# Softmax shifts of the second attention per half batch: maxima three head groups ahead, split on GpSimd

## What is computed

```python
q = x @ w_q + b_q                  # x: 16 batches, 256 queries, 128 channels
k = context @ w_k + b_k            # context: 1601 keys of 96 channels
v = context @ w_v + b_v
scores = einsum('bqhd,bkhd->bhqk', q, k) * 8 ** -0.5     # 16 heads of 8 channels
weights = softmax(scores, axis=-1)
out = einsum('bhqk,bkhd->bqhd', weights, v).reshape(16, 256, 128)
return out @ w_o + b_o
```

## Time and profile before

| | us |
|---|---|
| median of 3 runs | 2914.64 |
| lowest and highest run | 2913.44, 2914.93 |
| the profiled execution | 2913.21 |
| its span, first to last instruction | 2911.2 |
| VectorE busy | 2192.4 (75%) |
| TensorE busy | 2405.5 (83%) |
| ScalarE busy | 2106.3 (72%) |
| GpSimd busy | 1248.6 (43%) |

### The profile page before, as it was taken

One profiled execution on the slowest core, in us unless ns is written; L12 is line 12 of the kernel. 1 busy time (PEld: TensorE's weight loads), 2 busy tenths in 40 slices (PEclk: granted clock), 3 DMA queues, 4 the chain that ended last, 5 costly groups with the idle time before them and its releaser, 6 DMA issues. The chain is left out here.

```text
span 2911.2 us, 60895 instructions
## 1 busy us (share of the span) xinstructions
PE 2405.5 (83%) x19797; PEld 1252.2 (43%) x19797; DVE 2192.4 (75%) x8041; ACT 2106.3 (72%) x3547; POOL 1248.6 (43%) x1593
## 2 busy tenths in 40 slices
PE   7958888888888888667788479999999999999638
PEld 5735555555555555534522123333333333333337
DVE  8739878888888878636645799999999999993313
ACT  5749889898988888714412058888999888889325
POOL 1428777777777777713200412222322222200154
PEclk9979889988998899788888579999999999999669
DMA  8820000000000000081341113344443433330222
GB/s 245 266 79 12 13 14 15 14 13 14 13 18 19 14 15 14 5 290 55 51 117 35 68 49 104 89 98 108 106 104 95 105 89 97 95 68 2 59 93 68
DMA packets 163460, 205.76 MB, mean 71 GB/s; under 512 B 78588, under 2 KB 131106, under 8 KB 163126
## 3 DMA queue, kind: packets, MB, share of 16 engines
q1 hardware_dynamic: 152774, 161.80, 21.6%
q0 software_dynamic: 10352, 39.92, 4.0%
HBM read 135.19 MB, written 66.60 MB: 69 GB/s over the span
## 5 line engine op out<-in xcount | busy, mean ns | idle before, releaser
L2148 ACT ACTIVATE pb<-sps 128x512 f32<-128x512 f32 (+1 forms) x1664 | 896.1, 597 | 187.9 <-PE sps L2090 174.0
L2173 DVE TENSOR_REDUCE mx<-wps 128x2 f32<-128x1024 f32 x768 | 885.4, 1217 | 41.3 <-PE wps L2063 32.3
L1076 DVE MAX8 cand<-sc 128x8 f32<-128x46 f32 (+1 forms) x4480 | 602.7, 199 | 136.8 <-issue 77.9
L2105 PE MATMUL ops<-pb,va 128*9 128x256 f32 x6656 | 515.5, 382 | 8.2 <-issue 2.8
L852 PE MATMUL scores<-ctxT,qT 97*128 97x512 f32 (+1 forms) x1024 | 437.2, 576 | 80.5 <-ACT sc L964 69.5
L852 PEld LDWEIGHTS scores<-ctxT,qT 97*128 97x128 f32 x1024 | 206.6, 212 | 318.4 <-issue 218.6
L1943 POOL COPY va<-XX 128x128 f32<-128x128 f32 (+1 forms) x208 | 49.9, 292 | 626.0 <-PE ops L2105 618.4
L735 POOL TENSOR_TENSOR prf<-sc,prf 128x1601 f32<-128x1601 f32 x64 | 229.7, 3589 | 127.0 <-ACT prf L971 127.0
L827 PE MATMUL misc<-diag,prs 128*128 128x128 f32 (+1 forms) x1664 | 237.9, 300 | 7.0 <-issue 5.9
L735 POOL TENSOR_TENSOR prs<-sc,prs 128x1601 f32<-128x1601 f32 x64 | 230.6, 3604 | 16.8 <-ACT prs L971 13.8
L827 PEld LDWEIGHTS misc<-diag,prs 128*128 128x128 f32 (+1 forms) x1664 | 217.1, 207 | 17.3 <-issue 13.9
(11 more groups left out here) (407 smaller groups left out, 3953.5 us busy)
## 6 DMA issues: line engine op xcount, KB each, us to landing
FO<-keys SPq DMA_DIRECT2D x392, 50.0 KB
XX<-keys SPq DMA_DIRECT2D x392, 50.0 KB
ctxn<-in_ctx_dram SPq DMA_DIRECT2D x32, 576.0 KB
keys<-kpb POOLq DMA_DIRECT2D x42, 400.2 KB, 3.8
toep<-kernpad SPq DMA_DIRECT2D x8, 2048.0 KB, 14.9
values<-s_vs SPq DMA_DIRECT2D x16, 832.0 KB, 5.9
XX<-values SPq DMA_DIRECT2D x16, 832.0 KB, 4.8
keysf<-s_kf SPq DMA_DIRECT2D x16, 800.5 KB, 3.7
```

The source lines that it names most:

```text
L1076: st.add(v.max(cand[s % 2][:, 8 + n:8 + n + 7 * NP + 1:NP], sc[s % 4][:, c:c + w]))
L2105: ins = t.matmul(ops[VW * i:VW * i + DH1 + 1, 0:S], va[par][0:kn(kt), kt, 4 * g + i, :], pb[(UNITS * g + 2 * kt + i % 2) % 8][0:kn(kt), i ...
L2148: nc.scalar.activation(pb[(UNITS * g + u) % 8][0:rows_, :, :], sps[(UNITS * g + u) % SB][0:rows_, :, :], ACT.Exp).then_inc(p_ready, 1)
L2173: v.tensor_reduce(mx4[:, m // 2, :, 2 * g + m % 2, c], both, AX.X, ALU.max).then_inc(work_read, 1)
```

## The change

The maxima run three head groups ahead of the scores. In a batch's first group these are the last group of the same batch, in its other groups the first three of the next one; three groups of maxima run ahead of batch 0 and the last three groups of batch 15 have none beside them. The shifts are put in per half batch (two head groups): a half's split starts at the beginning of a batch's second group (for its own second half) and of its fourth group (for the next batch's first half), and one guard job stands at key tile 5 of each. VectorE only reduces `mx4` to `mneg` (half as many elements); the three casts and two subtractions are GpSimd's. TensorE turns both 128-query halves in one job, VectorE copies them to `mT` in one instruction of 256 columns on 24 partitions, and SyncE writes and reads back half the rows, twice per batch. In GpSimd's queue the split of a batch's second half stands between the spreading of the values and the splitting of the keys, the next one behind the splitting of the keys. In SyncE's queue the guard of the second half stands ahead of a batch's first loads. The scores wait for guard rows at the first and at the third group of a batch. Ahead of the loop, the split stands at the start of the third group and its guard job behind the fifth of that group's 13 jobs.

```diff
-                    mg = (g + 1) % HG
-                    ahead = 1 if g < HG - 1 else 2
-                    beside = follow >= ahead
-                    if g == HG - 1 and follow >= 1:
-                        do.split_maxima(b + 1)
+                    mg = (g + 3) % HG
+                    ahead = 0 if g == 0 else 1
+                    beside = ahead == 0 or follow
+                    half = 2 * b + (g + 1) // 2
+                    guarded = g == 1 or (g == 3 and follow)
+                    if guarded:
+                        do.split_maxima(half)
...
-                        if g == HG - 1 and follow >= 1 and kt in (5, 6):
-                            job(do.guard, b, par, b + 1, kt - 5)
+                        if guarded and kt == 5:
+                            job(do.guard, b, par, half)
...
-            for g in range(HG + 1):
+            for g in range(3):
                 for n in range(MJ):
-                    if g == HG and n == MJ // 2:
+                    if g == 2 and n == 0:
                         do.split_maxima(0)
-                    num = g * MJ + n
-                    do.maxima(g // HG, g // HG, 1, *job_args(g % HG, n), n == 0, num, wps[num % 2])
-            for q in range(2):
-                num = (HG + 1) * MJ + q
-                do.guard(0, q, num, wps[num % 2])
+                    num = g * MJ + n + (1 if g == 2 and n >= 5 else 0)
+                    do.maxima(0, 0, 1, *job_args(g, n), n == 0, num, wps[num % 2])
+                    if g == 2 and n == 4:
+                        do.guard(0, num + 1, wps[(num + 1) % 2])
...
+            def split_maxima(half):
+
+                pool.wait_ge(mneg_ready, half + 1)
+                pool.sem_inc(pool_passed, 1)
+                rest = mneg[:, :, :, :]
+                for n in range(3):
+                    st.link(g_.tensor_copy(mparts[:, :, n, :, :], rest))
+                    if n < 2:
+                        st.link(g_.tensor_tensor(rest, rest, mparts[:, :, n, :, :], ALU.subtract))
+                st.restart()
+                pool.sem_inc(mparts_ready, 1)
...
+            split_maxima(0)
+            split_keys(2)
+            split_maxima(1)
+            split_keys(3)
+            split_maxima(2)
+            for b in range(1, B - 1):
+                spread_values(b + 1, (b + 1) % 2)
+                split_maxima(2 * b + 1)
+                if b + 3 < B:
+                    split_keys(b + 3)
+                split_maxima(2 * b + 2)
+            split_maxima(2 * B - 1)
...
             def batch(b, par):
 
+                guard(2 * b + 1)
                 for g in range(HG - 2):
                     load(b + 2, par, g)
                 load_values(b + 2, True)
-                guard(b + 1, 1 - par, not (isinstance(b, int) and b == 0))
+                guard(2 * b + 2)
                 for g in range(HG - 2, HG):
                     load(b + 2, par, g)
...
-                if g == 0 and kt == 0:
-                    pe.wait_ge(guard_in, 32 * (b + 1))
+                if g % 2 == 0 and kt == 0:
+                    pe.wait_ge(guard_in, 32 * (2 * b + g // 2 + 1))
...
-            def split_maxima(b):
+            def split_maxima(half):
 
                 dve.wait_ge(work_read, maxima.last + 1)
-                rest = mneg[:, :, :, :]
-                st.link(v.tensor_reduce(rest.rearrange("p q o h -> p (q o h)"),
-                                        mx4[:, :, :, :, :].rearrange("p q o h c -> p (q o h) c"), AX.X, ALU.max, negate=True))
-                for n in range(3):
-                    st.link(v.tensor_copy(mparts[:, :, n, :, :], rest))
-                    if n < 2:
-                        st.link(v.tensor_tensor(rest, rest, mparts[:, :, n, :, :], ALU.subtract))
-                dve.sem_inc(mparts_ready, 1)
+                pairs = mx4[:, :, :, HP * (half % 2):HP * (half % 2) + HP, :]
+                v.tensor_reduce(mneg[:, :, :, :].rearrange("p q o h -> p (q o) h"),
+                                pairs.rearrange("p q o h c -> p (q o) h c"), AX.X, ALU.max, negate=True
+                                ).then_inc(mneg_ready, 1)
```

More of the change, by code:

```diff
@@ L1842, in base @@
                 return START
-            return START + PER * b - 3 - (MJ if isinstance(b, int) and b == B - 1 else 0)
+            return START + PER * b - 3
         def job_slot(b, par, n):
@@ L1893, in batch @@
                                 job(do.output, b, par, b - 1)
-                        if g == HG - 1 and follow >= 1 and kt in (5, 6):
-                            job(do.guard, b, par, b + 1, kt - 5)
+                        if guarded and kt == 5:
+                            job(do.guard, b, par, half)
                 do.batch_end()
-            for g in range(HG + 1):
+            for g in range(3):
                 for n in range(MJ):
-                    if g == HG and n == MJ // 2:
+                    if g == 2 and n == 0:
                         do.split_maxima(0)
-                    num = g * MJ + n
-                    do.maxima(g // HG, g // HG, 1, *job_args(g % HG, n), n == 0, num, wps[num % 2])
-            for q in range(2):
-                num = (HG + 1) * MJ + q
-                do.guard(0, q, num, wps[num % 2])
-            do.batch_end()
[L1910 to L1916, removed]
+                    num = g * MJ + n + (1 if g == 2 and n >= 5 else 0)
+                    do.maxima(0, 0, 1, *job_args(g, n), n == 0, num, wps[num % 2])
+                    if g == 2 and n == 4:
+                        do.guard(0, num + 1, wps[(num + 1) % 2])
+            do.batch_end()
+            batch(0, 0, {0: 1, 1: 1}, True, 1)
+            for i in range((B - 2) // 2):
+                batch(2 * i + 1, 1, {0: i + 1, 1: i + 2}, False, 1)
+                batch(2 * i + 2, 0, {0: i + 2, 1: i + 2}, False, 1)
+            batch(B - 1, 1, {0: B // 2}, False, 0)
             for kt in range(KT - LAG, KT):
@@ L2006, in load_values, with guard @@
                              k.values[bass.ds(b, 1), :, :].rearrange("o p c -> (o p) c")).then_inc(vn_in, 16)
[L2008 to L2015, removed]
+            def guard(half):
+                if half >= 2:
+                    sp.wait_ge(guard_in, 32 * (half - 1))
+                sp.wait_ge(mT_ready, half + 1)
+                rows_ = k.guards[half % 2][0:6 * HP]
+                sp.dma_start(rows_, mT[:, :, :].rearrange("r h p -> r (h p)")).then_inc(mT_saved, 16)
+                sp.wait_ge(mT_saved, 16 * (half + 1))
+                src = rows_.rearrange("(n o h) c -> o n h c", n=3, o=2)
+                first = 2 * HP * (half % 2)
                 for odd in range(2):
                     r = ROWS * odd + GUARD
-                    sp.dma_start(qs[par][r:r + 3, odd:H1:2, :], src[odd]).then_inc(guard_in, 16)
+                    sp.dma_start(qs[half // 2 % 2][r:r + 3, first + odd:first + 2 * HP:2, :], src[odd]).then_inc(guard_in, 16)
             for b in range(2):
                 load_values(b, b == 1)
-            guard(0, 0, False)
+            guard(0)
             def batch(b, par):
+                guard(2 * b + 1)
                 for g in range(HG - 2):
@@ L2037, in _ @@
             batch(B - 3, 1)
-            guard(B - 1, 1, True)
-            sp.wait_ge(guard_in, 32 * B)
+            for half in range(2 * B - 3, 2 * B):
+                guard(half)
+            sp.wait_ge(guard_in, 64 * B)
         @block.tensor
@@ L2065, in maxima, with guard @@
                 ins.then_inc(work_ready, 1)
-            def guard(b, q, job, buf):
-                pe.wait_ge(mparts_ready, b + 1)
-                if isinstance(b, int) and b == 0:
+            def guard(half, job, buf):
+                pe.wait_ge(mparts_ready, half + 1)
+                if half == 0:
                     pe.wait_ge(identb_ready, 1)
@@ L2073, in guard @@
                 pe.sem_inc(pe_passed, 1)
-                t.transpose(buf[0:3 * H1, 0:P // 2].bitcast(BF16), mparts[:, q, :, :, :].rearrange("p n o h -> p (n o h)"),
-                            identb[:, :]).then_inc(work_ready, 1)
+                turned = buf[0:6 * HP, 0:P].bitcast(BF16)
+                for q in range(QT):
+                    ins = t.transpose(turned[:, q * P:q * P + P], mparts[:, q, :, :, :].rearrange("p n o h -> p (n o h)"),
+                                      identb[:, :])
+                ins.then_inc(work_ready, 1)
             def scores(b, par, g, kt, first):
-                if g == 0 and kt == 0:
-                    pe.wait_ge(guard_in, 32 * (b + 1))
+                if g % 2 == 0 and kt == 0:
+                    pe.wait_ge(guard_in, 32 * (2 * b + g // 2 + 1))
                 for i in range(2):
@@ L2177, in maxima, with guard @@
                 maxima.last = job
-            def split_maxima(b):
+            def split_maxima(half):
                 dve.wait_ge(work_read, maxima.last + 1)
-                rest = mneg[:, :, :, :]
-                st.link(v.tensor_reduce(rest.rearrange("p q o h -> p (q o h)"),
```

(20 more changed lines are left out.)

22 lines of the change are left out of this document (7 added, 15 removed).

## The result

The change makes the kernel faster by a little more than was forecast: 2868.91 us (median of 4 runs, 2862.02 to 2870.32) against 2914.78 us for the kernel before on the same chip, a ratio of 0.9845 with a 95% interval of 0.9828 to 0.9863. The forecast was 2870.7 us, in a range of 2860 to 2888 us. The profiled execution of the changed kernel took 2868.78 us, its span 2866.8 us.

The account below looks back on a forecast made before the run. VectorE was taken to bound the second attention, with TensorE and ScalarE close below. Head start -35.0 us and loop -8.9 us sum to -43.9 us, taking the 2914.64 us median to 2870.7 us; range 2860 to 2888 us.

Parts of the forecast that it names:

- VectorE sets the pace: Second attention: VectorE is busy 14.22 of 14.40 us in a plain group; TensorE and ScalarE are not far below.
- The head start: Before the first exponential: three maxima groups instead of five, split off VectorE, transfers covered by eight maxima jobs; -35.0 us.
- The loop: From first to last exponential: -1.0 us per batch over 14 batches, less 5.1 us given back; -8.9 us.
- The guard job's 0.57 us: Each guard job in the loop delays VectorE's next maxima reduction by 0.57 us; a copy twice as wide stays inside it.
- Groups two and four: Sign in the changed profile: a batch's second and fourth head groups should be near 15.2 us.
- The end: Batches 14 and 15: two groups that ran without maxima now have them; +4.05 and +1.0 us, together +5.1 us.
- The loop's bound of -23 us: Best case over 14 batches: -1.6 us per batch if half of each guard copy's 0.57 us vanishes.
- GpSimd and SyncE in time: GpSimd's five small operations take 1.4 us against 5.6 us of jobs; moved queue work costs nothing while its cover holds.
- SyncE's meeting of the values' load and the second guard: Fourth group: the load lands up to 7.8 us in, the guard's write is issued at about 7.6 us; they just touch.
- the prediction's first rival: Guard transfers reach past their cover: each of 31 halves 0.3 us late, 9 us back, 2880 us; chance 0.08.
- TensorE was no bound: Rival: TensorE's 14.27 us in a plain group bounds it, so no gain per batch; 2884.7 us; chance 0.10.
- The slow side: Rival: the HBM round trip becomes the bound; 1.4 us late per half takes back everything, 2.4 gives 2945 us; chance 0.05.

Follow-up runs that it names:

- Three runs that added or removed work on VectorE: Split on GpSimd, kernel before: 2899.81 us; changed kernel with VectorE splitting, key split held back: 2902.83 us; changed kernel with two turning jobs per half: 2884.16 us.
- the merged job: Changed kernel without guard jobs: leftover-key job moved to sixth place in its group, taking the transposes into its free columns; 2836.05 us, ratio 0.9743.
- the order: Changed kernel with only the leftover-key job moved from last to sixth place of its group, separate guard jobs kept; 2852.48 us, ratio 0.979.
- the cover taken away: Changed kernel with the guard job ahead of the loop moved behind the third group's 13th job instead of the fifth; 2870.57 us.
- four writes: Changed kernel with the shifts written to device memory four times, one after the other, each waited for; 2918.67 us, ratio 1.0023.

## Why the prediction was right

**VectorE sets the pace.** Right. Three runs that added or removed work on VectorE moved the stage by about what was computed for it (-16.6 us for -17, +37.5 us for +40, +19.1 us for +17). Two came out otherwise, and each was taken apart by a further run: the halves with VectorE's split beside GpSimd's key split (+125.5 us for +40), and the merged job (-20.6 us for -8 to -11, half of it from the order).

**The head start.** Right, -35.5 us for -35.0. Its parts are there: two groups fewer, the split gone, the transfers covered. With the cover taken away, 4.7 us of it are lost again (the prediction had put 5 us on that).

**The loop.** Better than forecast, -13.3 us for -8.9. The mis-sized term is the reduction that stays on VectorE: 0.26 us each was put down, since it waits for the one before it; it costs 0.14 us (2129.25 to 2129.39 us), because the next maxima reduction no longer waits for it. With two of them per batch that is 0.24 us of the 0.31 us by which a batch came out better than forecast (62.49 us in place of 63.80, so -1.31 us for -1.0):

```profile
2128.53 0.69 DVE L2198 TENSOR_REDUCE mx<-wps 128x8 f32<-128x520 f32 x1
2129.25 0.22 DVE L2205 TENSOR_REDUCE mneg<-mx 128x16 f32<-128x64 f32 x1
2129.39 6.97 DVE L2195 TENSOR_REDUCE mx<-wps 128x2 f32<-128x1024 f32 x6
2136.28 0.27 DVE L2215 COPY mT<-wps 24x256 bf16<-24x256 bf16 x1
2136.85 6.88 DVE L2195 TENSOR_REDUCE mx<-wps 128x2 f32<-128x1024 f32 x6 [0.30 <-PE wps L2082]
```

The guard job's 0.57 us (2136.28 to 2136.85) is the predicted number, with a copy twice as wide. Groups two and four were said to come out near 15.2 us; they are 15.09 and 15.60, and the fourth has the 0.63 us of the batch's change in it, which the sum had kept and that sentence had left out. The end cost +4.7 us for +5.1. (The loop's bound of -23 us should read -22: 14 x 1.6 is 22.4.)

**The sum was nearer than its terms.** Those 4.4 us of extra gain and 4.1 us by which the stages ahead ran longer in the profiled execution cancel. That was luck. Whether the medians, -45.9 us, lie near by the same luck can't be read, since only the profiled executions show the stages apart.

**GpSimd and SyncE in time.** Right: five operations of 0.19 to 0.22 us, no wait of TensorE for them. SyncE's meeting of the values' load and the second guard did take place: in batch 7 the read-back was issued 2.92 us behind the write (1.35 us in the head start), and the slack held it: the copy ends 7.2 to 7.4 us before the scores that need it, where the prediction had worked out 7.0.

```profile
2159.95 1.48 SPq L2020 DMA_DIRECT2D XX<-values  x1
2166.32 0.31 SPq L2029 DMA_DIRECT2D guards<-mT  x1
2169.24 0.56 SPq L2035 DMA_DIRECT2D Y<-guards  x2
```

Four of 32 writes took over 2 us by this measure, so the high-load latency that the prediction's first rival drew on stayed the exception. That the values' load made them slow is not shown: two of the four belong to second halves, which have no values' load just ahead of them.

**The rivals.** Late transfers did not come, and TensorE was no bound at the groups' new length: the fourth came down with VectorE's work (17.60 to 15.60 us), the second went up by the work that it got (14.40 to 15.10 us), and without guard jobs they take 14.97 and 14.60 us. The slow side was priced too low. It put 43.9 us at 1.4 us of lateness per half; four writes had about that lateness, 45.7 us of waits in all, and lost 69 us, with TensorE's clock low behind 11 of the waits.

**What the prediction did not see.** It took moving the split off VectorE as 1 us per batch. Beside the halves it is worth far more. The halves with the split on VectorE and the key split out of its way gain 11.3 us (1085.1 - 1073.8: 34.2 us in the head start, of which the loop gives back 22.9), the move alone gains 16.6 us, both together 48.8 us: two splits per batch would cost VectorE twice. And with GpSimd's queue in its old order the halves would have lost 76.7 us, to VectorE's waits for GpSimd's instructions in the second group and the low clock behind them.

## What to carry to other kernels

When work is put in smaller portions, count its fixed chain as many times as there are portions, and take it off the pacing engine in the same step. When an operation moves to another time, look at what GpSimd does at that time: here a 0.17 us cast or subtraction of VectorE in SBUF waited for the end of a GpSimd cast or subtraction of 1.5 to 3.3 us. And measure a stage by its own first and last instruction: here the stages ahead moved by more than several of the effects.

## What the runs showed of the hardware

Not expected: a VectorE cast of 16 elements that took 3.67 us beside GpSimd's subtraction, 21 times its own 0.174 us. A wait of TensorE of 3.7 us that cost a second time, with the granted clock at 0.50 for the 9 us behind it. And a work buffer's turn as the price of a small job, 0.57 us with a copy of 0.21 us or 0.27 us alike, of which 0.34 us went away when the job shared another's buffer.
